# Last cross-attention stage of a decoder layer: expert weights' high parts, GpSimd's low parts, residuals and warming products put in other places

## What is computed

```
x = layernorm(x + linear_attention(x))          # Wq, Wk, Wv, Wg, Wp
x = layernorm(x + cross_attention(x, ctx_512))  # 16 heads, latent context of width 64
x = layernorm(x + experts(x))                   # 32 experts, inner width 96, top 8
```

## Time and profile before

| | us |
|---|---|
| median of 3 runs | 860.18 |
| lowest, highest | 859.62, 860.51 |
| the profiled execution's own time | 858.95 |
| its span, first to last instruction | 857.2 |
| PE busy | 830.4 (97%) |
| DVE busy | 637.9 (74%) |
| ACT busy | 280.0 (33%) |
| POOL busy | 182.0 (21%) |

### The profile page before, as it was taken

One profiled execution on the slowest core, in us unless ns is written; L12 is line 12 of the kernel. 1 busy time (PEld: TensorE's weight loads), 2 busy tenths in 40 slices (PEclk: granted clock), 3 DMA queues, 4 the chain that ended last, 5 costly groups with the idle time before them and its releaser, 6 DMA issues.

```text
span 857.2 us, 15916 instructions
## 1 busy us (share of the span) xinstructions
PE 830.4 (97%) x6312; PEld 666.5 (78%) x6312; DVE 637.9 (74%) x1395; ACT 280.0 (33%) x500; POOL 182.0 (21%) x152
## 2 busy tenths in 40 slices
PE   8999999999999999999899999999999999999995
PEld 6967678876887768876577878888888888887884
DVE  5677698899888998887867866666665657566586
ACT  5431252204432144311544423332422333232242
POOL 3036500563006620264512201200000000000120
PEclk9999999999999999999999999999999999999998
DMA  9310000100001000000220052201012021000011
GB/s 352 120 38 2 3 2 12 51 2 5 2 13 50 3 5 2 24 3 30 96 74 25 1 143 72 79 0 64 33 46 67 0 92 37 25 1 0 2 50 49
DMA packets 12836, 35.85 MB, mean 42 GB/s; under 512 B 1504, under 2 KB 2272, under 8 KB 12384
## 3 DMA queue, kind: packets, MB, share of 16 engines
q1 hardware_dynamic: 12768, 34.92, 11.8%
HBM read 30.26 MB, written 2.36 MB: 38 GB/s over the span
## 4 chain that ended last, share of the span: by engine, by line
PE 47%; DVE 4%; issue 1%; ACT 0%; POOL 0%; ACTq 0%; DVEq 0%
PE ps L256 14%; PE ps L258 14%; PE ps L257 14%; PE ps L1620 2%; PE ps L1611 1%; DVE su L541 1%; DVE h_lo L371 1%; DVE x2T_all L535 1%; PE ps L1594 0%; PE ps L634 0%; PE ps L1522 0%; DVE fst L506 0%; PE ps L1468 0%; POOL roped L778 0%; PE ps L324 0%
## 5 line engine op out<-in xcount | busy, mean ns | idle before, releaser
L778 POOL TENSOR_TENSOR roped<-prod 128x512 f32<-128x512 f32 x96 | 121.3, 1287 | 233.3 <-DVE prod L1105 233.3
L541 DVE TENSOR_TENSOR su<-sg,ps 128x512 f32<-128x512 f32 x96 | 65.9, 687 | 122.7 <-PE ps L258 119.5
L256 PE MATMUL ps<-y_hi,f_hi 128*128 128x512 f32 x384 | 151.2, 394 | 1.3 <-issue 1.3
L258 PE MATMUL ps<-y_hi,f_lo 128*128 128x512 f32 x384 | 149.5, 389 | 0.0
L257 PE MATMUL ps<-y_lo,f_hi 128*128 128x512 f32 x384 | 149.4, 389 | 0.0
L398 ACT ACTIVATE sg<-ps 128x512 f32<-128x512 f32 x96 | 57.3, 598 | 251.4 <-PE ps L258 251.3
L1105 DVE TENSOR_TENSOR prod<-ps,ropeq 128x512 f32<-128x512 f32 x192 | 118.7, 681 | 24.7 <-PE ps L258 22.5
L256 PEld LDWEIGHTS ps<-y_hi,f_hi 128*128 128x128 f32 x384 | 72.1, 188 | 16.8 <-issue 2.2
L257 PEld LDWEIGHTS ps<-y_lo,f_hi 128*128 128x128 f32 x384 | 72.1, 188 | 15.2 <-issue 0.5
L258 PEld LDWEIGHTS ps<-y_hi,f_lo 128*128 128x128 f32 x384 | 72.1, 188 | 15.1
L256 PE MATMUL ps<-xT_hi,a_hi 128*128 128x512 f32 x192 | 78.7, 410 | 3.7 <-DVE prod L1105 2.1
(11 more groups left out here) (178 smaller groups left out, 1328.0 us busy)
## 6 DMA issues: line engine op xcount, KB each, us to landing
cb<-routing SPq DMA_DIRECT2D x32, 256.0 KB
f_raw<-in_L_ffn_gate_up_proj SPq DMA_DIRECT2D x8, 768.0 KB, 6.3
f_raw<-in_L_ffn_down_proj SPq DMA_DIRECT2D x8, 384.0 KB, 7.3
xb<-in_x SPq DMA_DIRECT2D x4, 512.0 KB, 4.2
lq<-in_L_xattn_Wq SPq DMA_DIRECT2D x1, 2048.0 KB, 14.2
x2T_all<-in_L_xattn_Wo SPq DMA_DIRECT2D x1, 2048.0 KB, 12.0
x2T_all<-x2T SPq DMA_DIRECT2D x4, 512.0 KB, 3.3
roped<-in_L_xattn_w_kc_q SPq DMA_DIRECT2D x1, 1536.0 KB, 9.9
```

The costliest lines, as they stand in the source:

```text
L256: pe.matmul(dst, l_hi, r_hi, start=first, stop=False, skip_group_check=check)
L258: return pe.matmul(dst, l_lo, r_hi, start=False, stop=last, skip_group_check=check)
L541: dve.tensor_tensor(su[:, k % 2], sg[:, k % 2], bank(2 * (k % 2) + 1), ALU.mult).then_inc(s_su, 1)
L778: pool.tensor_tensor(roped[:, 2 * (t % 4) + k], made(2 * t + k)[:, 0], made(2 * t + k)[:, 1], ALU.add)\
```

## The change

On SyncE, the load of the first experts' weights stands ahead of the waits for the rope stage, behind a wait for all self-attention projections (`s_pj`). On ScalarE, the wait for that load, the three parts of `f_hi` and `y_hi` of block 0 move from the last cross stage into the last rope stage, ahead of `lq_out` of the last two pairs, with a wait for the last q_big products. On GpSimd, the low parts of the weights wait for the normalised weights of tile 0 (parts 0 to 2) and of tile 1 (parts 3 to 5), and the low parts of blocks 1 and 2 for those of tiles 2 and 3. On VectorE, the residual of tile 0 stands behind the normalisation of tile 2, and that of tile 1 behind that of tile 3. On TensorE, three and two warming products behind scores(2) and scores(3) go away, and two each are put between the halves of turn(0), behind turn(0), and between the halves of turn(1).

```
@@ SyncE, ffn_sync
+        sp.wait_ge(s_pj, 8 * BLOCKS)
+        load(0, 0)
         sp.wait_ge(s_qr, SLOTS * BLOCKS)
         sp.wait_ge(s_q, 24 * BLOCKS)
         sp.wait_ge(s_kept, 32 * LAST + 1)
-        load(0, 0)
         for n in range(LAST):
             store_c(n)
@@ GpSimd, cross
             else:
-                for n in range(LAST):
+                y_lo_out(pool, 0)
+                for part in range(F_PARTS):
+                    if part % 3 == 0:
+                        pool.wait_ge(s_nrm, 8 * b + 2 + 2 * (part // 3))
+                    f_lo_part(pool, 0, 0, part)
+                for n in range(1, LAST):
+                    pool.wait_ge(s_nrm, 8 * b + 4 + 2 * n)
                     y_lo_out(pool, n)
-                    for part in range(F_PARTS if n == 0 else 0):
-                        f_lo_part(pool, 0, 0, part)
@@ ScalarE, pairs
+            if not following:
+                act.wait_ge(s_fload[0], 32)
+                act.wait_ge(s_q, 24 * BLOCKS)
+                for part in range(3):
+                    f_hi_out(act, 0, part)
+                y_hi_out(act, 0)
             lq_out(b, PAIRS - 2)
             lq_out(b, PAIRS - 1)
@@ ScalarE, cross
                 for m in range(LAST):
                     cT_out(act, m)
-                y_hi_out(act, 0)
                 expo(0)
                 turned(0)
-                act.wait_ge(s_fload[0], 32)
-                f_hi_out(act, 0, 0)
                 expo(1)
-                f_hi_out(act, 0, 1)
                 context(0)
-                f_hi_out(act, 0, 2)
                 expo(2)
@@ VectorE, cross
                 shift(b, 2)
+                normalise(b, 2)
                 residual2(b, 0, 6)
-                normalise(b, 2)
                 shift(b, 3)
+                normalise(b, 3)
                 residual2(b, 1, 6)
-                normalise(b, 3)
                 norm2(b, 0)
@@ TensorE, cross
-            def turn(t):
+            def turn(t, warm=0):
                 for p in range(PAIRS):
+                    if p == 4:
+                        keep_warm(warm, 7)
@@ TensorE, cross
                 scores(b, 1)
-                turn(0)
+                turn(0, 2)
+                keep_warm(2, 7)
                 context(0)
                 scores(b, 2)
-                keep_warm(3, 7)
-                turn(1)
+                turn(1, 2)
                 project(0)
                 context(1)
                 scores(b, 3)
-                keep_warm(2, 7)
                 turn(2)
```

## The result

The changed kernel takes 861.57 us (median of 10 runs, 860.56 to 862.39), the kernel before, run beside it, 859.40 (10 runs, 858.95 to 860.51). The ratio is 1.0023, with a 95% interval of 1.0014 to 1.0031: some 2 us slower (the quotient of the two medians alone is 1.0025), a hair over the 0.2% that the prediction took as the limit of what can be told. The ten times of the kernel before lie in two groups, six from 858.95 to 859.62 us and four from 860.18 to 860.51. The two profiled executions lie further apart than the medians (862.17 and 858.95, spans 860.4 and 857.2), since the one of before was among its fastest and the one of after among its slower ones; inside the stage the two are offset by only 0.1 us (the kept routing's DMA at 399.74 and 399.85).

A forecast was written before the change was run, and what follows sets the result against it. The prediction took TensorE, busy for 97% of the span, as the bound. Its terms summed to +0.1 us with the clock at 2.4 GHz, plus 1.5 for the clock: +1.6, 861.8 us against the median; range 859.5 to 864.4.

The forecast's parts named there:

- A: Rival on TensorE: clock low in the empty gap and back before context(0), +1.0 to +2.4 us, 861.2 to 862.6; chance 0.45.
- Step 1: ScalarE and SyncE: expert load issued no earlier than 400.2 us, lq_out(6) starts at 408.8 instead of 404.34, +4.5 us.
- Step 2: GpSimd's y_lo clear of VectorE's first product by the reciprocals, -0.92 us; the f_lo waits cost nothing.
- Step 3: TensorE's context(0) runs at 2.4 GHz with warming in both gaps, 1.72 us for 3.55, -1.83 us.
- Step 4: TensorE's warming behind the scores taken out, -1.49 and -1.06 us, with 0.92 put into turn(1); -1.63 us in all.
- Step 6: TensorE's clock low from about 409.5 to 413 us, behind 4.4 us quite empty before scores(1); +1.5 us.
- the sum with the clock at 2.4 GHz: At turn(2) on TensorE: 4.5 - 0.92 - 1.83 - 1.63 = +0.1 us.
- Step 5: VectorE's residuals behind the normalisation buy slack and no time; SyncE's later routing rows cost nothing; zero.
- main case: A, chance 0.45, about half of it on either side of +1.7 us.
- Rival E: Early load not held by SyncE's queue, landing before lq_out's input (404.2): +0.1 - 4.5 us, 855.8 us; chance 0.12.

The follow-up runs named there:

- fill_gap: The changed kernel with 18 products of ones put where TensorE waits for the late lq_out; 860.00 us, ratio 1.0001 to the kernel before.
- fix_no_pool: fix_sync with GpSimd's waits for s_nrm taken away; 856.33 us, ratio 0.9958 to the kernel before.
- act_back: The changed kernel with ScalarE's part alone undone, f_hi and y_hi of block 0 back in the cross stage; 857.17 us, ratio 0.9965 to the kernel before.
- pe_only: The kernel before with TensorE's part alone, the warming products moved; 859.11 us, ratio 0.9991 to the kernel before.
- fix_no_dve: fix_sync with residual2 of tiles 0 and 1 ahead of the normalisations again; 855.74 us, ratio 0.9952 to the kernel before.
- act_only: The kernel before with ScalarE's and SyncE's part alone; 863.55 us, ratio 1.0040 to the kernel before.
- fix_sync: The changed kernel with the first expert load issued ahead of keep_c(2) on SyncE; 855.67 us, ratio 0.9948 to the kernel before.
- fix_cold0: fix_sync with the four warming products in and behind turn(0) taken out; 856.77 us, ratio 0.9960 to the kernel before.

## Why the prediction was right

The direction and the mechanism held, and the time lies close to the forecast: +1.6 us and 861.8 were forecast, 0.0023 of 859.4, about 2.0 us, and 861.57 were measured; of the rivals it was A, the clock low from the empty gap on and back before context(0).

Part of the closeness is luck. The +1.6 us were worked out for turn(2) and for the profiled execution, which was to take 860.6 us with turn(2) at 430 to 431. It took 862.17, and turn(2) began at 431.81, 2.9 us later than before without the offset of 0.1; that is beyond the +2.4 that A allowed. The 861.8 came from adding 1.2 us for the median of three runs, 860.18, and ten runs gave 859.40. Where the missing 1.3 us are can be read with fill_gap: 0.2 in steps 1 and 2 (context(0) at 418.26 for 418.1), 0.4 in steps 3 and 4, 0.7 in step 6. Step by step:

- Step 1 held. Issue 400.36 for 400.2, ScalarE's start at 406.00 for 405.65, lq_out at 409.16 for 408.8. The 0.35 us are the first half's issue, 0.60 us and not 0.33, and the offset of 0.1.
- Step 2 held: 0.69 us. fix_no_pool and act_back show that it is GpSimd's subtraction beside the product that costs. Left out was its worth at tile 1, where the products of act_back and pe_only pay 0.4 to 0.8 us each (1.15, 1.08 and 1.50 us for 0.69).
- Step 3 held but for 0.2 us: it priced the context products at 1.72 us, and the scores behind them start 1.92 us after their first (420.58 to 422.50).
- Step 4 was right on what goes and too large by 0.2 us. In fill_gap, with the clock at 1.00, turn(2) begins 11.3 us behind the first context product (418.26 to 429.55 in its chain of waits), where steps 3 and 4 leave 14.33 - 1.83 - 1.63 = 10.9. So the sum with the clock at 2.4 GHz, +0.1, is +0.7 in that profile (429.55 for 428.84), though by its median times fill_gap is where the kernel before is.
- Step 5 held in the time, as far as fix_no_dve shows it with the load early.
- Step 6 is the mis-sized one. The fall came where it was put, at 409.2 for 409.5, but I took the length from the kernel before, 3.4 us, and it was 6.8. The "+1.5" of the prediction measured 1.9 us by fill_gap's times and 2.2 by its profile. It is tempting to say that thin work behind the gap, scores and turn_c, kept the clock low; act_only has the same work there and 3.4 us. What sets the length stays open.

The prediction put half of its main case on either side of +1.7 us, and the result fell just beyond it. Rival E, the faster one, asked for the load to be free of SyncE's queue: fix_sync made that so and gave 3.9 us at turn(2) (4.4 had been priced) and 0.0052 of 860 us, 4.5 us, in the time.

## What to carry to other kernels

An issue moved up in a program starts only when the queue ahead of it lets it: look for the last wait above its new place (here the routing store at 399.74), not at its own semaphore. A copy put ahead of one on the critical path must have its input there already; here ScalarE's idle time would have held all of it, and moving one pair of DMAs turned 0.23% slower into 0.52% faster. Parts of a schedule change that win together can win little alone (pe_only), so take them out one by one from the version that works. And a forecast made on one profile is to be held against a profile of the result as well as against the median: here the median hid 1.3 us of error.

## What the runs showed of the hardware that I had not expected

The lower clock lasted 6.8 us behind an empty stretch of 4.5 and 4.7 us in the two profiles of the changed kernel, and 3.4 us in the kernel before behind a stretch with transposes in it; in act_only, behind an empty stretch of 4.5 us, it was over by 413.0, after 3.4 us, and it fell anew at 419.8. A length of a clock fall taken from one row is thus not the length of the next, and these runs do not show what decides between the two. And it fell, in fix_cold0, with eight transposes inside the thin stretch, in some executions of one and the same kernel. By the idle rule of the Trainium skill ("TensorE: Matmul & The Clock Gate", Part 1) alone, as the prediction read it, thin work would be harmless; the prediction held the trace of before against that, and fix_cold0 and act_only (its fall at 419.8, with transposes in the stretch ahead of it) bear it out.
